# Macaron block on one Trainium2 core: weight casts of the last tile earlier, one layer-norm job later, first ternary pieces cut and reordered

## The reference

```python
x = x + 0.5 * ffn(layernorm(x))        # ffn 0
x = x + attention(layernorm(x))        # 16 heads, 4 kv heads, 128 wide, causal, rotary
x = x + 0.5 * ffn(layernorm(x))        # ffn 1, same weights as ffn 0

def ternary_quant(w):                  # W_up, W_gate, W_down
    scale = mean(abs(w)) + 1e-8
    return clip(round(w / scale), -1, 1) * scale
def ffn(x):
    return (silu(x @ wu.T) * (x @ wg.T)) @ wd.T     # 256 -> 1024 -> 256
```

## Time and profile before

| | us |
|---|---|
| median of 3 runs | 1106.16 (1105.7 to 1106.87) |
| time of the profiled execution | 1105.64 |
| its span, first to last instruction | 1103.9 |
| busy: PE / DVE / ACT / POOL | 1074.5 / 940.7 / 809.1 / 704.7 |

### The profile page before, as it was taken

One profiled execution on the slowest core, in us unless ns is written; L12 is line 12 of the kernel. 1 busy time (PEld: TensorE's weight loads), 2 busy tenths in 40 slices (PEclk: granted clock), 3 DMA queues, 4 the chain that ended last, 5 costly groups with the idle time before them and its releaser, 6 DMA issues.

```text
span 1103.9 us, 26841 instructions
## 1 busy us (share of the span) xinstructions
PE 1074.5 (97%) x8521; PEld 847.3 (77%) x8521; DVE 940.7 (85%) x2337; ACT 809.1 (73%) x2020; POOL 704.7 (64%) x876
## 2 busy tenths in 40 slices
PE   7999997899999999999999999999999998999998
PEld 4556654688888888888888888888888886566665
DVE  6798887799999999999999999999999996433433
ACT  4687986588787787877878878888787784444443
POOL 2465665477677777777777777777777773444444
PEclk9999999899999999999999999999999999999999
DMA  9432331144343344343443434334434343100101
GB/s 348 139 58 40 58 58 23 37 80 79 69 86 67 71 84 78 71 81 71 81 81 71 76 67 91 67 71 81 81 71 81 71 81 68 30 19 19 38 19 38
DMA packets 262134, 79.93 MB, mean 72 GB/s; under 512 B 249296, under 2 KB 260816, under 8 KB 261840
## 3 DMA queue, kind: packets, MB, share of 16 engines
q1 hardware_dynamic: 261664, 79.19, 34.3%
q10 hardware_dynamic: 432, 0.27, 0.1%
HBM read 12.85 MB, written 4.19 MB: 15 GB/s over the span
## 4 chain that ended last, share of the span: by engine, by line
PE 74%; issue 9%; DVE 6%; POOL 6%; ACT 4%; DMA 1%; POOLq 0%; DVEq 0%; ACTq 0%
PE bank L688 46%; PE bank L748 14%; POOL SCR L388 5%; PE bank L657 5%; PE bank L677 4%; PE bank L649 4%; ACT SCR L573 1%; DVE ARENA L1058 1%; DMA SCR<-ARENA 1%; ACT SCR L465 1%; DVE SCR L889 1%; ACT ARENA L580 1%; DVE bank L1038 1%; DVE ST L836 0%; DVE SCR L1019 0%
## 5 line engine op out<-in xcount | busy, mean ns | idle before, releaser
L414 POOL TENSOR_SCALAR SCR<-SCR,RI 128x128 f32<-128x128 f32 (+1 forms) x512 | 309.5, 604 | 44.0 <-DVE RI L1054 3.8
L399 POOL TENSOR_TENSOR SCR<-SCR 128x512 f32<-128x512 f32 x160 | 203.1, 1269 | 156.7 <-DVE SCR L1019 148.4
L573 ACT ACTIVATE SCR<-bank,NM 128x128 f32<-128x128 f32 (+1 forms) x512 | 208.6, 420 | 125.2 <-DVE NM L1038 125.2
L388 POOL TENSOR_TENSOR SCR<-SCR 128x512 f16<-128x512 f32 x128 | 152.0, 1188 | 173.7 <-ACT SCR L480 172.7
L545 ACT COPY SCR<-bank 64x512 f32<-64x512 f32 x320 | 185.6, 580 | 21.6 <-PE bank L688 15.4
L748 PE MATMUL bank<-SCR 128*128 128x128 f32 (+1 forms) x1024 | 193.7, 332 | 2.5 <-ACT SCR L573 2.5
L1058 DVE TENSOR_TENSOR ARENA<-SCR,ARENA 128x768 f16<-128x768 f32 x128 | 187.8, 1467 | 4.4 <-ACT ARENA L580 3.4
L688 PE MATMUL bank<-WOH,ARENA 128*128 128x256 f16 x1024 | 188.5, 273 | 2.2 <-DVE ARENA L1049 1.3
L889 DVE SCALAR_TENSOR_TENSOR SCR<-SCR,CS,bank 128x512 f32<-128x512 f32 x128 | 95.2, 744 | 112.0 <-PE bank L657 103.5
L1038 DVE CUSTOM_DVE_ANT_0 bank<-bank,MASK,SCQ 128x128 f32<-128x128 f32 (+1 forms) x512 | 182.9, 417 | 0.8
L488 ACT ACTIVATE SCR<-bank,SU 128x512 f32<-128x512 f32 x128 | 87.7, 685 | 117.3 <-PE bank L649 117.3
(11 more groups left out here) (115 smaller groups left out, 1654.4 us busy)
## 6 DMA issues: line engine op xcount, KB each, us to landing
out<-X SPq DMA_DIRECT2D x7, 512.0 KB, 2.9
X<-in_x SPq DMA_DIRECT2D x1, 2560.0 KB, 10.0
ARENA<-in_wq SPq DMA_DIRECT2D x1, 2048.0 KB, 13.9
ARENA<-in_wo SPq DMA_DIRECT2D x1, 2048.0 KB, 18.9
SCR<-ARENA SPq DMA_TRANSPOSE x128, 3.6
X<-in_x SPq DMA_DIRECT2D x3, 512.0 KB, 9.6
X<-in_wu SPq DMA_DIRECT2D x1, 1024.0 KB, 6.7
X<-in_wg SPq DMA_DIRECT2D x1, 1024.0 KB, 8.9
```

The source lines that it names most:

```text
L388: gp.tensor_tensor(HL[:, f % 4, :], H32[:, f % 2, :], HH[:, f % 4, :], ALU.subtract).then_inc(s["hl_done"], 1)
L399: gp.tensor_tensor(dst, M1[:, m, :], M2[:, m, :], ALU.add).then_inc(add, 1)
L414: last = gp.tensor_scalar(EX[:, par, lo:hi], EX[:, par, lo:hi], RI[:, par, c:c + 1], PS, ALU.mult, ALU.mult)
L573: last = act.activation(EX[:, par, 384 * hh + lo:384 * hh + hi], SBK[hh][:, lo:hi], ACT.Exp, bias=NM[:, par, c:c + 1], scale=-1.0, accum_o ...
```

## The change

It has five parts. (1) W_up and W_gate are each loaded in two DMAs of 512 KB, and their absolute values are summed in halves (two ACT instructions each, added by PE by accumulating two matmuls); the second total stands inside the first `up`, with 4 instead of 8 filling matmuls ahead. (2) The first quarters of W_up and W_gate are made in halves of 128 channels, both first halves before the second ones, and `TERNARY` spreads the other quarters anew. (3) Norm job 1 moves: bias, centring, high and low part from pieces 1, 2, 3, 3 to 2, 3, 4, 5. (4) In tile 7 the casts move to pieces (0, 0, 1, 2) on ACT and (1, 2, 2, 4) on DVE; PE waits for 14 of 16 behind the last `gate` and for all 16 only ahead of the first V projection. Job 14's bias, centring, high and low part come one piece earlier. (5) Job 15 moves from batch 0 to batch 1: statistics, root at (1, 0), bias at (1, 1), centring at (1, 2), now on ACT, high part at (1, 3), low part and transpose at (1, 4).

```diff
-        TERNARY = {-1: [(0, 0), (1, 0)], 0: [(0, 1), (1, 1), (0, 2)], 1: [(2, 0)], 2: [(2, 1), (1, 2)], 4: [(0, 3), (1, 3)],
+        TERNARY = {-1: [(0, 0), (1, 0)], 0: [(0, 1), (1, 1)], 1: [(2, 0), (0, 2)], 2: [(1, 2)], 3: [(2, 1), (0, 3)], 4: [(1, 3)],
                    5: [(2, 2)], 7: [(2, 3)]}
+        CAST_HI = [(2, 2, 5, 6)] * 3 + [(0, 0, 1, 2)]
+        CAST_LO = [(2, 5, 6, 7)] * 3 + [(1, 2, 2, 4)]
-        norm_job(1, 1, -1, 1, 2, 3, 3)
+        norm_job(1, 1, -1, 2, 3, 4, 5)
-                norm_job(2 * n, n - 1, at + 3, at + 5, at + 6, at + 6, at + 7)
+                norm_job(2 * n, n - 1, at + 3, at + 4, at + 5, at + 5, at + 6)
...
-            sp.dma_start(RU, wu.rearrange("(c p) e -> p c e", p=P)).then_inc(ffn_raw[0], 16)
-            sp.dma_start(RG, wg.rearrange("(c p) e -> p c e", p=P)).then_inc(ffn_raw[1], 16)
+            for i, (raw, w) in enumerate(((RU, wu), (RG, wg))):
+                for c in range(DC):
+                    sp.dma_start(raw[:, c * E:(c + 1) * E], w[c * P:(c + 1) * P, :]).then_inc((ffn_raw, ffn_raw2)[c][i], 16)
...
+            absolute(0, 0)
+            absolute(0, 1)
+            first_hi(0)
+            absolute(1, 0)
+            first_hi(1)
+            absolute(1, 1)
...
-                pe.matmul(FTOT[i], ONES[:, :], PSUMS[:, i:i + 1], start=True, stop=True).then_inc(f_tot, 1)
+                for c in range(halves):
+                    last = pe.matmul(FTOT[i], ONES[:, :], PSUMS[:, 2 * i + c:2 * i + c + 1], start=c == 0, stop=c == halves - 1)
...
-                making = layer == 0 and isinstance(n, int) and n == 0 and f % 2 == 0
+                making = layer == 0 and isinstance(n, int) and n == 0 and (f % 2 == 0 or f == 1)
+                pieces_of = 1 + f if f < 2 else f // 2 + 2
...
-                        pe.wait_ge(w_ready, 4 * len(CUTS))
+                        pe.wait_ge(w_ready, 3 * len(CUTS) + 2)
...
                         if isinstance(b, int) and b == 0:
                             pe.wait_ge(ln_x[0], 16 * (TILES - 1))
+                            pe.wait_ge(w_ready, 4 * len(CUTS))
...
                 if f == -1:
                     for i in range(2):
                         ternary_scale(i)
-                        ternary_piece(i, 0)
+                        ternary_piece(i, 0, 0)
                         if i == 0:
                             first_lo()
+                    for i in range(2):
+                        ternary_piece(i, 0, 1)
                 else:
+                    if f == 1:
+                        ternary_scale(2)
                     for i, q in TERNARY[f]:
                         ternary_piece(i, q)
-                if f == 0:
-                    ternary_scale(2)
...
-                    if isinstance(b, int) and (b, i) == (0, 1):
+                    if isinstance(b, int) and (b, i) == (1, 0):
                         ve.wait_ge(ff[0]["x_done"], SUB * TILES)
                         stats(2 * TILES - 1, TILES - 1)
-                    if isinstance(b, int) and (b, i) == (0, 2):
-                        center(2 * TILES - 1, TILES - 1, XN7)
+                    if isinstance(b, int) and (b, i) == (1, 1):
+                        norm_bias(2 * TILES - 1)
+                    if isinstance(b, int) and (b, i) == (1, 4):
+                        norm_lo(2 * TILES - 1, XN7)
```

More of the change, by code:

```diff
@@ L156, in program @@
         ffn_raw = [sem(f"ffn_raw{i}") for i in range(3)]
+        ffn_raw2 = [sem(f"ffn_raw_second{i}") for i in range(2)]
         attn_raw, hs_in, tab_in = sem("attn_raw"), sem("hs_in"), sem("tab_in")
@@ L450, in _, with first_hi, norm_center @@
             act.dma_start(SIN[:, :], sin_t).then_inc(tab_in, 16)
[L452 to L457, removed]
+            def first_hi(c):
+                act.wait_ge(ln_t0, c + 1)
+                act.copy(x_tile(0, 0, c), TB[c][:, :].rearrange("p (t n) -> p t n", t=2)).then_inc(ln_xh0, 1)
+            def norm_center(q, tile, rows=XN):
                 act.wait_ge(ln_nb, q)
@@ L464, in norm_center @@
                 for s in range(SUB):
-                    act.activation(XN[:, s // 2, :, s % 2, :], X[:, tile * (SUB * D) + s * D:tile * (SUB * D) + (s + 1) * D].rearrange("p (c d) -> p c d", c=DC),
+                    act.activation(rows[:, s // 2, :, s % 2, :], X[:, tile * (SUB * D) + s * D:tile * (SUB * D) + (s + 1) * D].rearrange("p (c d) -> p c d", c=DC),
                                    ACT.Identity, bias=NB[:, s:s + 1], scale=RSTD[:, s:s + 1]).then_inc(ln_xn, 1)
@@ L490, in ffn @@
                         act.wait_ge(ffn_raw[2], 16)
-                        act.activation(flat(TD), RD, ACT.Abs, accum_out=PSUMS[:, 2:3]).then_inc(f_part[2], 1)
+                        act.activation(flat(TD), RD, ACT.Abs, accum_out=PSUMS[:, 4:5]).then_inc(f_part[2], 1)
                     if f > 0:
@@ L513, in weights @@
                         act.mul(RO[:, h * D:(h + 1) * D], RO[:, h * D:(h + 1) * D], HS[:, h:h + 1]).then_inc(hs_mul, 1)
-                for i, piece in enumerate((2, 2, 5, 6)):
-                    if n >= CUT0 and f == piece:
+                for i in range(len(CUTS)):
+                    if n >= CUT0 and f == CAST_HI[n - CUT0][i]:
                         act.wait_ge(a_sc, 1)
@@ L529, in _, with absolute @@
             act.activation(WARM[:, 0:1], NEGHALF[:, 0:1], ACT.Silu)
[L530 to L534, removed]
+            def absolute(i, c):
+                raw, t = ((RU, TU), (RG, TG))[i]
+                act.wait_ge((ffn_raw, ffn_raw2)[c][i], 16)
+                act.activation(t[:, c, :], raw[:, c * E:(c + 1) * E], ACT.Abs, accum_out=PSUMS[:, 2 * i + c:2 * i + c + 1]).then_inc(f_part[i], 1)
+            absolute(0, 0)
[4 more added lines that the diff above has]
+            absolute(1, 1)
             act.wait_ge(f_sc, 1)
@@ L591, in batch @@
                         rows_hi(ends(b))
-                    if isinstance(b, int) and (b, i) == (0, 3):
+                    if isinstance(b, int) and (b, i) == (1, 2):
+                        norm_center(2 * TILES - 1, TILES - 1, XN7)
+                    if isinstance(b, int) and (b, i) == (1, 3):
                         norm_hi(2 * TILES - 1, *turned_ahead(2 * TILES - 1), XN7)
@@ L623, in total @@
                     pe.wait_ge(f_sc, 1)
-                pe.wait_ge(f_part[i], 1)
-                pe.matmul(FTOT[i], ONES[:, :], PSUMS[:, i:i + 1], start=True, stop=True).then_inc(f_tot, 1)
+                halves = (2, 2, 1)[i]
+                pe.wait_ge(f_part[i], halves)
+                for c in range(halves):
+                    last = pe.matmul(FTOT[i], ONES[:, :], PSUMS[:, 2 * i + c:2 * i + c + 1], start=c == 0, stop=c == halves - 1)
+                last.then_inc(f_tot, 1)
             def largest():
@@ L646, in up @@
                     if making and f == 0:
+                        if a == 1:
+                            total(1)
                         pe.wait_ge((ln_xh0, ln_xl0)[a], 2)
@@ L721, in _ @@
             total(0)
-            keep_warm(8)
-            total(1)
+            keep_warm(4)
             ffn(0, 0, False)
@@ L807, in batch @@
                     if real(b, i, 5):
-                        if isinstance(b, int) and (b, i) == (0, 5):
+                        if isinstance(b, int) and (b, i) == (1, 7):
                             pe.wait_ge(ln_x[1], 16 * TILES)
@@ L839, in stats, with center @@
                     ve.bn_aggr(MV[:, s, :], ST[:, s, :]).then_inc(ln_mv, 1)
-            def center(q, tile, rows=XN):
+            def center(q, tile):
                 ve.wait_ge(ln_rs, q + 1)
[L843 to L846, removed]
                 for s in range(SUB):
-                    ve.tensor_scalar(rows[:, s // 2, :, s % 2, :], X[:, bass.ds(tile * (SUB * D) + s * D, D)].rearrange("p (c d) -> p c d", c=DC),
+                    ve.tensor_scalar(XN[:, s // 2, :, s % 2, :], X[:, bass.ds(tile * (SUB * D) + s * D, D)].rearrange("p (c d) -> p c d", c=DC),
                                      MV[:, s, 0:1], RSTD[:, s:s + 1], ALU.subtract, ALU.mult).then_inc(ln_xn, 1)
@@ L926, in weights @@
                     scales()
-                for i, at in enumerate((2, 5, 6, 7)):
-                    if n >= CUT0 and f == at:
+                for i in range(len(CUTS)):
+                    if n >= CUT0 and f == CAST_LO[n - CUT0][i]:
                         raw, hi, lo, size, c = CUTS[i]
```

26 lines of the change are left out of this document (14 added, 12 removed).

## The result

The changed kernel takes 1103.41 us (1103.19 to 1104.81, 12 runs) where the kernel before, run beside it, takes 1105.86 (1105.55 to 1107.2): ratio 0.9979, 95% interval 0.9971 to 0.9988. It is faster by 2.45 us, not by the 5.1 of the forecast. The profiled execution took 1104.81 (span 1103.0) and is the longest of the twelve; eight of them lie between 1103.19 and 1103.44.

The account below looks back on a forecast made before the run. PE was busy 97%, so time hung on its few waits and on DVE's pace in attention; casts 7.7 - start 2.1 - job 15 0.5 = 5.1 us, from 1106.16 to 1101.1, range 1096.0 to 1105.0.

Parts of the forecast that it names:

- Casts of tile 7: Tile 7 and the pass to attention: PE's wait and slow K matmuls go, a later residual costs 1.2; 7.7 us gained.
- Start: Tile 0 and head of tile 1, parts 1 to 3: costs 2.1 us, bounds 4 and nothing.
- the transpose is issued at 31.40 + 4.85 = 36.25: Tile 0: DVE work added ahead of job 1's low part delays its transpose by 4.85 us; it lands at 40.55.
- PE could start tile 1 at about 37.2: End of tile 0: shorter PE waits and the new order would make PE ready at 37.2 instead of 40.18.
- the term of 1.65 us: Head of tile 1: lower clock behind PE's wait costs 3.5 x 0.47 = 1.65 us.
- 4.5 us to spare: Old start: job 1's transpose lands at 35.7, 4.5 us before tile 1's first `up` at 40.18.
- Job 15: Attention, job 15 moved from batch 0 to batch 1: 5.0 us gained, 5.5 lost, costs 0.5 net.
- A: Rival at the start: job 1's low part comes early enough, tile 1 starts at 37.2; +3.0 instead of -2.1, 1096.0; chance 0.14.
- B: Rival in tile 7: two stops drop the clock, 1.65 more, and DVE's WQL stretches by 1.1; 1103.9; chance 0.13.
- C: Rival in (1, 2): Identity needs table loads, there and back to Exp, 2.6 us more on ACT; 1103.7; chance 0.04.
- D: Rival in attention: ACT's backlog of (1, 3) persists, eight pairs each 1.3 late; +8.2 us, 1109.3, slower; chance 0.06.
- E: Rival in batch 0: everything won at the pass is only waited for again; 1106; chance 0.06.

Follow-up runs that it names:

- casts_only: The kernel before with part 4 alone (casts of tile 7, job 14 a piece earlier, wait for 14 of 16): 1098.08 us, ratio 0.9928.
- wq_low_later: start_undone with DVE's low part of WQ in tile 7 moved behind the residual of tile 6: 1097.73 us, ratio 0.9928.
- small_pool: The changed kernel with POOL's subtractions of pieces 0 to 5 of tile 0 on 4 of 512 columns, the rest left out: 1098.92 us.
- warm_wait: The changed kernel with sixteen filling matmuls in PE's wait for job 1's transpose ahead of tile 1: 1102.04 us, ratio 0.9964.
- start_undone: The changed kernel with parts 1 to 3 undone, so parts 4 and 5 remain: 1097.47 us, ratio 0.9921 against the kernel before.
- start_only: The kernel before with parts 1 to 3 only: 1111.94 us, ratio 1.0053.
- late_norm: start_undone with job 1's bias, centring, high and low part at pieces 2, 3, 4, 5: 1105.14 us.
- job1_back: The changed kernel with norm job 1 back at pieces 1, 2, 3, 3: 1101.31 us, ratio 0.9952 against the kernel before.
- order_only: start_undone with only the new order of the ternary quarters, kept whole, job 1 in its old place: 1098.96 us.

## Why the prediction was right and wrong

**Casts of tile 7: right.** Forecast 8.9 - 1.2 = 7.7. In the traces the deficit of 6.2 at the second `up` of tile 1 is a lead of 1.6 at the last `down` of the FFN (196.86 against 198.45): 7.8. Wait, clock and stall came as told and in their places. In the runs it is 8.3 (casts_only). In the trace of casts_only the lead at that `down` is 8.4 (190.01 against 198.45), but 0.6 of it stands already at tile 1 (39.55 against 40.18), in code that is the same in both kernels and ran at a lower clock in the one before; the casts bring the same 7.8. So the size came out right partly by luck: the stall that I priced at 1.2 costs nothing (wq_low_later), and what holds the gain below 8.9 is DVE's rotary at the pass, for which PE waits there instead, and which the sum did not have.

**Start: right sign, wrong size. This is the step that failed.** Forecast: a cost of 2.1, at most 4; measured 5.9. Two of its terms were too small, the time of the transpose and the 0.4 us by which it makes tile 1 late, and the clock behind them with it.

*When the transpose goes out.* The sum "the transpose is issued at 31.40 + 4.85 = 36.25" contained no stretch beyond those of the kernel before, and without any the runs show 34.51 (small_pool): its base of 31.40 already held two, about 1.7 us together (1.52 and 1.11 instead of 0.75 and 0.15). Of those the changed kernel has six. Their excess over the clean durations (0.75, 0.75, 0.15, 0.48, 0.48, 1.22) is 0.98 + 0.77 + 0.96 + 0.63 + 0.24 + 0.96 = 4.5 us, and 34.5 + 4.5 and the 0.35 by which its tile 0 had begun later give 39.4 (measured: 39.38). I had seen the long bias beside a subtraction of POOL, but booked the stretches only as the upper bound of 4, by an estimate, and left them out of the likeliest sum. What follows from it: "PE could start tile 1 at about 37.2" took 3 us of PE's waits in tile 0 as gone, but PE waits for the same stretched DVE, 0.22, 0.46, 0.81 and 1.16 us, and ended tile 0 at 39.7. The DMA landed at 43.9 instead of 40.55. The clock: the wait was 4.17 instead of 3.3 us, and the slow stretch 5.05 instead of 3.5, which was only the width of the windows in the earlier trace rows. So no run shows the term of 1.65 us; in its place stand the 2.45 us of the trace (at 0.50) and the 1.4 between the medians of the changed kernel and warm_wait.

*How late that makes tile 1.* The forecast had the head of tile 1 late by 0.4, the landing at 40.55 set against 40.18. But 40.18 is a start with the old order's own meetings with POOL in it. Without them it is 36.43 in the old start and 39.04 in the new: 2.6 late, although the transpose is 5.5 later, near the +4.85 of the sum. The "4.5 us to spare" were in part PE's own delay. By the medians, 1.6 of the 3.8 us above the forecast are stretches that the new start has beyond the old one, and 2.2 stay without any (4.3 against 2.1); how much of these is clock is open, since in the two profiled executions without them, with the clock up, the start costs 2.8.

*The meetings.* In the six rows DVE's instruction ends behind POOL's, five times by 0.01 to 0.55 us (the low part, twice as long, by 1.08): 20.75 + 1.73 = 22.48 against 20.78 + 1.15 = 21.93; 33.28 + 1.11 = 34.39 against 32.95 + 1.16 = 34.11. What was left of POOL's instruction when DVE's began is 1.18, 0.98, 1.10, 0.83, 0.44 and 1.10 us, each 0.14 to 0.21 more than the excess above. POOL's record need not begin first: in the first meeting DVE's begins 0.03 us ahead of it, and is the long one all the same. The h, which reads a PSUM bank, took 0.72 to 0.74 in tile 0, beside POOL's subtractions too (32.62 and 35.09). So the price of a meeting was about the rest of POOL's instruction, here 0.24 to 0.98 us, and I argue that meetings come oftener as DVE's idle times close: I had booked the closing of two such gaps (0.46 and 0.48) as a gain only. That the denser list is why there are six meetings instead of two is argued, not shown.

**Job 15: mechanism right, sign wrong.** Forecast: batch 0 gains 5.0, batch 1 costs 5.5. Comparing start_undone with casts_only, the probabilities' low part of the third pair starts at 215.59 instead of 220.18, 4.6 gained; in (1, 7) at 272.58 instead of 272.92, 4.3 lost; and in (2, 0) at 279.88 instead of 280.83, so 0.6 more is gained where the loop begins. Ahead of that DVE of casts_only idles 0.51 us for ACT's rotary copy, and that of start_undone does not. Net +0.9 in the traces at that point and +0.6 in the runs, against -0.5. The term that was too large is batch 1's, 5.5 against 4.3: the late pairs seem to share one backlog of ACT, where I had added their delays one to the other. That is argued, not shown.

**The rivals.** A (the start gains) is excluded by start_only. B (a slow clock in tile 7, WQL stretched) did not come: WQL took 1.27, and the clock was 1.00 behind the stop at the first `down` (182.7 to 186.2 us) and at K. C: no table load; there are three in the whole kernel, as before, and none beside the centring (Identity) at 250.46. D: the backlog of ACT did not carry over into batch 2. E: the lead from the pass survived. None of them held what happened: a start three times as dear as forecast. The time of 1103.4 lies in the range, near its upper end of 1105.0, but not for its reasons: that end was drawn for B, for C and for a start that costs 4, which alone would give 1103.0. It is in by luck. The start cost 3.8 more than forecast, and two errors the other way, 0.6 of the casts and 1.1 of job 15, hide part of it.

## What to carry to other kernels

Count meetings, not averages: where one engine sets the pace and another's work stretches its instructions (here by 0.24 to 0.98 us a meeting), list the other's instructions over the new timetable and add the rest of each to the sum, first as the likeliest value and not as a bound; take those of the old timetable out of the base. Do so on both sides of a slack: 4.5 us between a landing and its use are not there to be spent when part of them is delay of the user, which the same account would take away. And a wait that moves to the head of a stage where PE sets the pace can cost the clock as well (0.50 behind the 4.17 us here, 2.45 us of the trace). Undo one part at a time: here two parts brought 8.9 us (start_undone, 1097.47, the fastest kernel that computes the whole reference), and the other three gave 5.9 of them back. (The difference, 3.0, is 0.6 above the 2.45 measured directly; the kernel before stood at 1106.4 beside the one and at 1105.9 beside the other.)

## What the hardware showed that was not expected

The clock does not fall by the length of the wait alone. Behind waits of 4.17, 3.97 (late_norm) and 7.42 us it was at 0.50, 0.50 and 0.61; behind 2.71 us (small_pool's profiled execution) it stayed at 1.00. And the same wait in the same place can go either way: behind 1.94 us in piece 6 it fell to 0.50 in job1_back (39 to 41 us) and stayed at 1.00 in order_only, and behind 2.07 us it fell to 0.53 in the kernel before and stayed at 1.00 in start_undone:

```profile
28.50 1.04 PE L662 MATMUL bank<-XX,TG 128*128 128x512 f16 x4 [2.07 <-DVE TG L960]
```

and the window behind it, with the granted clock after the count of matmuls:

```profile
28.45:31.95 3.50, 3.45 (x20) 1.00 0.33 106
```

And POOL pays in these meetings too: a subtraction that takes 1.16 us elsewhere took 1.47 and 1.72 in the rows above. POOL's subtractions of pieces 0 to 5 in tile 0 are worth 2.9 us of the whole kernel in the old start and 4.5 in the new one, though no matmul and no DVE instruction in these timelines waits for one of them.
